# Ten embedding tables on one core: loads of five tiles of x, and pairs of tiles in the last table

## The chip, the cores and the metric

The kernel runs on one core of a Trainium2 chip. The metric is the device time of one execution in microseconds. Before the change it is 276.47 us, the median of three runs (276.41 to 276.67).

## The reference

Ten inputs x0 to x9 (1024 rows, 12500 down to 100 columns, float32) are multiplied by ten tables w0 to w9 (as many rows, 64 columns). The output holds, side by side, a factorization term over all tables and the ten products.

```python
embs = [jnp.dot(x, w) for x, w in zip(xs, ws)]
emb_sum = embs[0]
q_emb = jnp.dot(xs[0] ** 2, ws[0] ** 2)
for i in range(1, len(xs)):
    emb_sum = emb_sum + embs[i]
    q_emb = q_emb + jnp.dot(xs[i] ** 2, ws[i] ** 2)
fm_ans = 0.5 * (emb_sum ** 2 - q_emb)
return jnp.concatenate([fm_ans] + embs, axis=-1)
```

The elements of x are zeros and ones, nearly all of them zeros.

## The kernel before

x is kept transposed: a table with v rows is cut into tiles of 128 of them, and one tile of x is 128 partitions by the 1024 rows of the batch, 512 KB. There are 196 tiles. In memory the tiles of one table lie behind each other in each partition, so a load of n tiles is 128 rows of 4n KB each. The tiles go through a ring of 20 slots in SBUF (`x_ring`, `RING`, line 46).

`ORDER` (line 29) is written by hand. It names the tables in the order in which they are worked on (8, 9, 5, 4, 7, 3, 1, 6, 0, and 2 last), cuts each into groups of up to eight tiles, and each group into chunks of one or two tiles. A group is the unit in which w is loaded, squared and split into a high and a low part (`load_w`, `square` on ScalarE, lines 360 and 368; the split on GpSimd, lines 468 and 470). A chunk is the unit of ScalarE and TensorE: `count_set` (line 373) turns a chunk of x into zeros and ones (`is_set`) and counts them, `multiply` (line 497) multiplies it by the low and the high part of [w, w squared], four matmuls of 512 columns for a tile. The last group's last two tiles (`H`) are loaded in halves of the batch and are `FINAL`: the first of them goes the usual way in two half chunks, the second through `multiply_last` (line 515, six bf16 matmuls) and through ScalarE at line 420.

`plan_counts` (line 128) makes the loads and counts. It joins chunks of one group to at most four tiles (`LOAD`, line 45; two in the last table). Each joined list is one `Count`: VectorE's `count_ones` (line 601) counts the ones in it with one instruction. It is also one `Load`, except in the last table, where each chunk has a load of its own, and the four half loads of `FINAL`. A load gets a place in the ring: behind the one before it, or at slot 0 where it does not fit before slot 20 any more (line 152). `load.free` (line 173) is the count up to which ScalarE and VectorE must have read before the place, and the landing semaphore, may be used again.

SP issues the loads of x in their order at line 327, each behind its wait at line 325, and the outputs of nine tables behind them at line 333. w is loaded by ScalarE's queue at line 365. ScalarE's instructions stand in the order of the chunks, with the squarings, the copies of finished sums (`copy_sums`, line 390) and of finished embeddings (`copy_emb`, line 395) between them. At most five chunks are between ScalarE and TensorE (`SETS`).

When the last chunk is multiplied, VectorE adds its sums to the total (line 629), TensorE transposes total and sums (lines 554 and 527), ScalarE and VectorE make the first output from them, and a flag says whether all elements were zeros and ones (lines 564 to 569 on TensorE, 650 and 653 on VectorE). All engines read that flag before the program ends.

Of the kernel before, what the change touches and what calls it, by code (L numbers as in the profile page):

```python
# [16 lines left out]
BATCH = 1024  # L17
# [8 lines left out]

H = "halves"
FULL = [2, 2, 2, 2]
ORDER = [
    (8, [[2]]),  # L30
    (9, [[1]]),
    (5, [[2]]),
    (4, [[2, 2, 1]]),
    (7, [[2, 2]]),
    (3, [FULL, [2]]),
    (1, [FULL] * 6 + [[1]]),
    (6, [FULL]),
    (0, [FULL] * 12 + [[2]]),
    (2, [FULL, [2, 1, 1, 1, 1], [1, 1, 1, 1, H]]),
]  # L40
LAST = ORDER[-1][0]
CHUNK = max(FULL)
GROUP = sum(FULL)

LOAD = 4
# [14 lines left out]
class Chunk:  # L60


    def __init__(self, k, table, tile, n, at, half=None):
        self.k, self.table, self.tile, self.n, self.at = k, table, tile, n, at

        self.halves = (0, 1) if half is None else (half,)
        self.first, self.width = (half or 0) * HALF, len(self.halves) * HALF
        self.group = self.count = None
# [22 lines left out]
class Group:  # L91


    def __init__(self, g, place, table, tile, sizes, k):
        self.g, self.place, self.table, self.tile = g, place, table, tile
        self.whole, self.pair = g % WHOLES, g % PAIRS
        self.chunks, at = [], 0
        for n in sizes:
            if n == H:
                n = 2  # L100
                for half in range(2):
                    self.chunks.append(Chunk(k + len(self.chunks), table, tile + at, 1, at, half))
            else:
                self.chunks.append(Chunk(k + len(self.chunks), table, tile + at, n, at))
            at += n
        for chunk in self.chunks:
            chunk.group = self
        self.tiles, self.end = at, k + len(self.chunks)
# [3 lines left out]
def plan():  # L112
    groups, k = [], 0
    for n, (table, lists) in enumerate(ORDER):
        tile = 0
# [12 lines left out]
def plan_counts():  # L128

    lists = []  # L130
    for group in GROUPS:
        joined = []
        for chunk in group.chunks:
            most = 2 if group.table == LAST else LOAD
            if joined and (sum(c.n for c in joined) + chunk.n > most or
                           len(chunk.halves) < len(joined[0].halves)):
                lists.append(joined)
                joined = []
            joined.append(chunk)
        lists.append(joined)  # L140
    loads, counts, at = [], [], 0
    for chunks in lists:
        one = chunks[0]
        if len(one.halves) == 1:
            parts = [(one.tile, 1), (one.tile + 1, 1)]
        elif one.table == LAST:
            parts = [(chunk.tile, chunk.n) for chunk in chunks]
        else:
            parts = [(one.tile, sum(chunk.n for chunk in chunks))]
        length = sum(n for _, n in parts) * BATCH  # L150

        at = 0 if at + length > RING * BATCH else at
        own = []
        for first in range(0, BATCH, one.width):
            for i, (tile, n) in enumerate(parts):
                here = at + first + sum(m for _, m in parts[:i]) * BATCH
                own.append(Load(len(loads) + len(own), one.table, tile, n, first, one.width, here))
        at += length
        counts.append(Count(len(counts), own, chunks))
        place = own[0].at  # L160
        for chunk in chunks:

            chunk.place, place = place, place + chunk.n * chunk.width
            chunk.load = max((load for load in own if load.at < place), key=lambda load: load.at)
        for load in own:
            load.count = counts[-1]
        loads += own
    counts[-1].loads.sort(key=lambda load: load.at)
    for load in loads:

        had = [other.count for other in loads[:load.i] if other.land == load.land or
               other.at < load.at + load.length and load.at < other.at + other.length]
        load.free = max([count.c + 1 for count in had] + [0])
    return loads, counts


LOADS, COUNTS = plan_counts()

FINAL = COUNTS.pop()
# [8 lines left out]
def due(k, after):  # L188

    return [n for n in range(NT - 1) if min(END[n] - 1 + after, NCHUNKS - 1) == k]  # L190


def rec_kernel(nc, xs, ws, out):
# [3 lines left out]
    with ExitStack() as ctx:  # L197
# [120 lines left out]
        def _(sp):  # L318
# [11 lines left out]

            for n, (t, _) in enumerate(ORDER[:-1]):
                sp.wait_ge(emb_copied, n + 1)
# [26 lines left out]
        def _(act):  # L359
# [33 lines left out]
            def copy_emb(n, t):  # L393
                act.wait_ge(sums_turned, n + 1)
                nc.scalar.activation(results[:, t + 1, :, :], turning(n), ACT.Copy  # L395
                                     ).then_inc(emb_copied, 1)
# [6 lines left out]
            for group in GROUPS:  # L403
                for c, chunk in enumerate(group.chunks):
# [8 lines left out]
                    for n in due(chunk.k, TAKE_AFTER):  # L413
                        copy_emb(n, ORDER[n][0])

# [302 lines left out]
```

## Time and profile before

| what | value |
|---|---|
| runs, median (lowest to highest) | 276.47 us (276.41 to 276.67) |
| the profiled execution: time, span | 276.46 us, 274.7 us |
| PE, DVE, ACT, POOL busy | 78%, 82%, 82%, 42% of the span |
| DMA | 113.92 MB, mean 415 GB/s |
| loads of x | 42 of 2048 KB, 9 of 1024 KB, 11 of 512 KB, 4 of 256 KB |
| a count of four tiles, VectorE | 4.42 us |
| a chunk of two tiles, of one tile, ScalarE | 1.91 us, 1.06 us |

The span is the time from the first to the last record of the profile; the execution is 1.8 us longer. The busy shares are means over the whole span: three engines and the transfers are all busy most of it, so the shares alone do not say which of them sets the time. The slices and the waits do.

### The profile page before, as it was taken

The numbers are of one execution on the slowest core, as the hardware profiler recorded it, in microseconds if no ns is written. First come the engines' busy times: TensorE is split into PE (matmuls) and PEld (weight loads), VectorE is DVE, ScalarE is ACT, GpSimd is POOL, SyncE is SP. The second block draws the span as 40 slices with busy tenths as digits, with TensorE's granted clock in tenths as the row PEclk, the third lists the DMA queues.
The fourth block names the chain that finished last, engine by engine and source line by source line (L and its number), as shares of the span: only waits on it lengthen the run. The fifth ranks groups of instructions, "written<-read, shape, count | busy, mean of one in ns | idle before, by whom it ended". The sixth has DMA issues, their size and how long they took to land.

```text
span 274.7 us, 2715 instructions
## 1 busy us (share of the span) xinstructions
PE 213.9 (78%) x891; PEld 151.0 (55%) x892; DVE 224.1 (82%) x136; ACT 224.7 (82%) x269; POOL 114.9 (42%) x82
## 2 busy tenths in 40 slices
PE   0529889699988867878887787788788688698995
PEld 0416566476756555656654555555555465466763
DVE  2676876888798798878978978987987897999985
ACT  1649998999988788899868878877877796899994
POOL 0446757585414109267235135045045051073922
PEclk9968999999999999999999999999999999999999
DMA  7999999999999999999999999999999999999997
GB/s 263 441 402 440 410 420 417 426 421 442 416 424 426 427 420 426 421 423 428 420 424 430 420 431 428 417 424 429 420 427 431 419 423 430 410 414 416 410 398 269
DMA packets 15710, 113.92 MB, mean 415 GB/s; under 512 B 2000, under 2 KB 3280, under 8 KB 9168
## 3 DMA queue, kind: packets, MB, share of 16 engines
q1 hardware_dynamic: 11088, 106.96, 92.9%
q10 hardware_dynamic: 4608, 6.79, 6.7%
q8 instruction: 7, 0.11, 0.2%
q14 instruction: 7, 0.06, 0.1%
HBM read 110.85 MB, written 2.88 MB: 414 GB/s over the span
## 4 chain that ended last, share of the span: by engine, by line
DMA 63%; ACT 13%; issue 12%; PE 7%; SPq 1%; POOL 1%; ACTq 1%; DVE 0%; POOLq 0%
DMA x_ring<-in_x_dram 58%; ACT is_set L379 9%; PE sums L510 6%; DMA whole<-in_w_dram 5%; ACT turned L390 2%; SPq L327 1%; ACT whole L371 1%; POOL total L481 1%; ACT results L395 1%; ACTq L365 1%; PE sums L520 0%; ACT L371 0%; PE sums L554 0%; POOL high L468 0%; PE sums L527 0%
## 5 line engine op out<-in xcount | busy, mean ns | idle before, releaser
L604 DVE TENSOR_SCALAR_CACHE_REDUCE is_one<-x_ring 128x4096 uint8<-128x4096 f32 (+2 forms) x59 | 219.6, 3732 | 45.9 <-DMA x_ring<-in_x_dram 44.4
L379 ACT ACTIVATE is_set<-x_ring 128x2048 fp32r<-128x2048 uint32 (+2 forms) x106 | 190.1, 1796 | 32.1 <-DMA x_ring<-in_x_dram 31.6
L510 PE MATMUL sums<-is_set,low 128*128 128x512 f32 x396 | 133.1, 417 | 57.8 <-ACT is_set L379 42.8
L510 PE MATMUL sums<-is_set,high 128*128 128x512 f32 x396 | 124.9, 396 | 0.0
L510 PEld LDWEIGHTS sums<-is_set,low 128*128 128x128 f32 x396 | 68.1, 190 | 97.7 <-ACT is_set L379 43.3
L468 POOL CAST high<-whole 128x1024 fp32r<-128x1024 f32 (+5 forms) x31 | 27.1, 874 | 140.9 <-ACT whole L371 140.9
L510 PEld LDWEIGHTS sums<-is_set,high 128*128 128x128 f32 x396 | 75.5, 191 | 17.5
L470 POOL TENSOR_TENSOR low<-whole,high 128x1024 fp32r<-128x1024 f32 (+5 forms) x31 | 60.8, 1961 | 2.5
L371 ACT ACTIVATE whole<-whole 128x512 f32<-128x512 f32 (+5 forms) x31 | 16.5, 535 | 7.3 <-DMA whole<-in_w_dram 7.3
L379 ACT ACTIVATION_READ_ACCUMULATOR is_set<-x_ring 128x1 f32 x106 | 19.8, 187 | 0.0
L481 POOL TENSOR_TENSOR total<-total,turned 128x1024 f32<-128x1024 f32 x8 | 19.2, 2398 | 0.0
L390 ACT ACTIVATE turned<-sums 128x1024 f32<-128x1024 f32 x9 | 9.1, 1016 | 0.4 <-issue 0.3
L527 PEld LDWEIGHTS sums<-identity,turned 64*128 64x128 f32 x80 | 5.8, 139 | 3.9 <-issue 3.5
L527 PE MATMUL sums<-identity,turned 64*128 64x64 f32 x80 | 7.3, 229 | 0.0
L371 ACT ACT_TABLE_LOAD x1 | 1.3, 1283 | 6.1 <-DMA whole<-in_w_dram 6.1
L395 ACT ACTIVATE results<-sums 128x512 f32<-128x512 f32 x9 | 5.3, 585 | 0.0
L491 POOL TENSOR_SCALAR is_one<-x_ring 128x1024 bf16<-128x1024 f32 x1 | 2.8, 2784 | 5.1 <-DMA x_ring<-in_x_dram 5.1
L604 DVE DVE_READ_ACCUMULATOR is_one<-x_ring 128x1 f32 x59 | 4.9, 83 | 0.0
L448 POOL TENSOR_SCALAR total<-total,weight 128x1024 f32<-128x1024 f32 x1 | 2.9, 2863 | 0.1
L465 POOL COPY results<-whole 128x128 f32<-128x128 f32 x1 | 0.3, 292 | 4.3 <-ACT whole L371 4.3
L429 ACT ACTIVATE turned<-sums 128x512 f32<-128x512 f32 x2 | 1.2, 595 | 0.9 <-DVE total L629 0.9
L629 DVE SCALAR_TENSOR_TENSOR total<-sums,weight,total 128x512 f32<-128x512 f32 x2 | 1.5, 750 | 0.1
(37 smaller groups left out, 13.7 us busy)
## 6 DMA issues: line engine op xcount, KB each, us to landing
x_ring<-in_x_dram SPq DMA_DIRECT2D x42, 2048.0 KB, 21.5
x_ring<-in_x_dram SPq DMA_DIRECT2D x9, 1024.0 KB, 19.1
x_ring<-in_x_dram SPq DMA_DIRECT2D x11, 512.0 KB, 17.8
whole<-in_w_dram ACTq DMA_DIRECT2D x21, 256.0 KB, 9.7
out_dram<-results SPq DMA_DIRECT2D x9, 256.0 KB, 9.1
x_ring<-in_x_dram SPq DMA_DIRECT2D x4, 256.0 KB, 14.3
whole<-in_w_dram ACTq DMA_DIRECT2D x2, 192.0 KB, 7.1
whole<-in_w_dram ACTq DMA_DIRECT2D x4, 64.0 KB, 8.8
```

Of the source, the lines that this page charges most:

```text
L371: nc.scalar.activation(w[:, 1], w[:, 0], ACT.Square).then_inc(squared, 1)
L379: nc.scalar.activation(is_set[chunk.k % SETS][:, 0:length], in_ring(chunk.place, length).bitcast(U32), ACT.Sign, accum_out=set_counts[:, c ...
L390: nc.scalar.activation(turned[n % 2][:, :].rearrange("p (a b) -> p a b", a=2), sums[:, at:at + 2, :], ACT.Copy).then_inc(sums_copied, 1)
L395: nc.scalar.activation(results[:, t + 1, :, :], turning(n), ACT.Copy).then_inc(emb_copied, 1)
L448: nc.gpsimd.tensor_scalar(total[:, :], total[:, :], weight[:, 0:1], None, ALU.mult).then_inc(total_weighted, 1)
L468: nc.gpsimd.tensor_copy(first, w).then_inc(high_ready, 1)
L470: nc.gpsimd.tensor_tensor(part_of(group, low), w, first.bitcast(F32), ALU.subtract).then_inc(parts_ready, 1)
L481: nc.gpsimd.tensor_tensor(total[:, :], total[:, :], turned[n % 2][:, :], ALU.add).then_inc(added, 1)
L491: nc.gpsimd.tensor_scalar(last_ones[:, 0:BATCH], in_ring(FINAL.at, BATCH), 1.0, None, ALU.is_equal).then_inc(masked, 1)
L510: last = nc.tensor.matmul(sums[:, summing(n, half), :], w, x[:, at:at + HALF], start=first, stop=False, skip_group_check=True)
L527: last = nc.tensor.transpose(turning(n)[:, b, :], turned[n % 2][0:D, b * P:(b + 1) * P], identity[0:D, 0:D])
L604: nc.vector.tensor_scalar(is_one[c % 2][:, to:to + length], in_ring(at, length), 1.0, None, ALU.is_equal, ALU.add, accum_out=one_counts[:, ...
```

## The change

`FIVE` is a new list of sizes. A group of that shape is loaded in one transfer of five tiles. Its chunks stay 2, 2, 1, and it has two counts, one of four tiles and one of the fifth. The tables 4, 3, 1 and 0, which left one or two tiles over when cut by four, get one or two such groups at their end: table 3 is two of them, table 1 ends in a group of four and one of five, table 0 in two of five. In the last table a list of chunks is one load now, so the four pairs of one-tile chunks are each loaded in one transfer. The number of groups stays 31; there are 108 chunks in place of 106, 61 counts in place of 59 and 58 loads in place of 66.

```diff
--- before.py
+++ after.py
@@ -26,16 +26,17 @@
 
 H = "halves"
 FULL = [2, 2, 2, 2]
+FIVE = [2, 2, 1]
 ORDER = [
     (8, [[2]]),
     (9, [[1]]),
     (5, [[2]]),
-    (4, [[2, 2, 1]]),
+    (4, [FIVE]),
     (7, [[2, 2]]),
-    (3, [FULL, [2]]),
-    (1, [FULL] * 6 + [[1]]),
+    (3, [FIVE, FIVE]),
+    (1, [FULL] * 5 + [[2, 2], FIVE]),
     (6, [FULL]),
-    (0, [FULL] * 12 + [[2]]),
+    (0, [FULL] * 11 + [FIVE, FIVE]),
     (2, [FULL, [2, 1, 1, 1, 1], [1, 1, 1, 1, H]]),
 ]
 LAST = ORDER[-1][0]
@@ -94,7 +95,7 @@
     def __init__(self, g, place, table, tile, sizes, k):
         self.g, self.place, self.table, self.tile = g, place, table, tile
         self.whole, self.pair = g % WHOLES, g % PAIRS
-        self.chunks, at = [], 0
+        self.chunks, self.sizes, at = [], sizes, 0
         for n in sizes:
             if n == H:
                 n = 2
@@ -143,10 +144,17 @@
         one = chunks[0]
         if len(one.halves) == 1:
             parts = [(one.tile, 1), (one.tile + 1, 1)]
-        elif one.table == LAST:
-            parts = [(chunk.tile, chunk.n) for chunk in chunks]
         else:
             parts = [(one.tile, sum(chunk.n for chunk in chunks))]
+        if one.group.sizes == FIVE and one.at:
+
+            load = counts[-1].loads[0]
+            counts.append(Count(len(counts), [load], chunks))
+            counts[-1].at, counts[-1].length = load.at + one.at * BATCH, BATCH
+            one.place, one.load, load.count = counts[-1].at, load, counts[-1]
+            continue
+        if one.group.sizes == FIVE:
+            parts = [(one.tile, sum(FIVE))]
         length = sum(n for _, n in parts) * BATCH
 
         at = 0 if at + length > RING * BATCH else at
@@ -157,6 +165,8 @@
                 own.append(Load(len(loads) + len(own), one.table, tile, n, first, one.width, here))
         at += length
         counts.append(Count(len(counts), own, chunks))
+        if one.group.sizes == FIVE:
+            counts[-1].length = LOAD * BATCH
         place = own[0].at
         for chunk in chunks:
```

The names in the rows below: `x_ring` is the ring, `in_x_dram` the inputs, `is_set` a chunk after ScalarE, `x_landed` the landing semaphores (`LANDS`, 16 of them by turns). 128x4096 is four tiles, 128x1024 one.

SP's queue, the loads of x, before:

```order
L327 DMA x_ring<-in_x_dram 128x2048
L327 DMA x_ring<-in_x_dram 128x4096 x12
L327 DMA x_ring<-in_x_dram 128x1024
L327 DMA x_ring<-in_x_dram 128x4096 x26
L327 DMA x_ring<-in_x_dram 128x2048 x6
L327 DMA x_ring<-in_x_dram 128x1024 x8
L327 DMA x_ring<-in_x_dram 128x512 x4
L333 DMA out_dram<-results 128x512 x9
```

and now:

```order
L337 DMA x_ring<-in_x_dram 128x5120 x2
L337 DMA x_ring<-in_x_dram 128x4096 x11
L337 DMA x_ring<-in_x_dram 128x5120
L337 DMA x_ring<-in_x_dram 128x4096 x24
L337 DMA x_ring<-in_x_dram 128x5120 x2
L337 DMA x_ring<-in_x_dram 128x2048 x9
L337 DMA x_ring<-in_x_dram 128x512 x4
L343 DMA out_dram<-results 128x512 x9
```

The loads of one and two tiles at the ends of the tables 3, 1 and 0 (and 4, further up) are gone into loads of five. The last table has nine loads of two tiles where it had five of two and eight of one.

ScalarE at the end of table 0 and the begin of the last table, before:

```order
L379 ACTIVATE is_set,set_counts<-x_ring 128x2048 [waits x_multiplied,x_landed15]
L371 ACTIVATE whole<-whole 128x512 [waits w_landed1]
L379 ACTIVATE is_set,set_counts<-x_ring 128x2048 [waits x_multiplied,x_landed15]
L379 ACTIVATE is_set,set_counts<-x_ring 128x2048 [waits x_multiplied,x_landed0]
L365 DMA whole<-in_w_dram 128x384 [waits parts_ready]
L371 ACTIVATE whole<-whole 128x384 [waits w_landed2]
L379 ACTIVATE is_set,set_counts<-x_ring 128x2048 [waits x_multiplied,x_landed1]
```

and now:

```order
L389 ACTIVATE is_set,set_counts<-x_ring 128x2048 [waits x_multiplied,x_landed10]
L389 ACTIVATE is_set,set_counts<-x_ring 128x2048 [waits x_multiplied,x_landed11] x2
L375 DMA whole<-in_w_dram 128x384 [waits parts_ready]
L389 ACTIVATE is_set,set_counts<-x_ring 128x1024 [waits x_multiplied,x_landed11]
L381 ACTIVATE whole<-whole 128x512 [waits w_landed1]
L389 ACTIVATE is_set,set_counts<-x_ring 128x2048 [waits x_multiplied,x_landed12] x2
L375 DMA whole<-in_w_dram 128x384 [waits parts_ready]
L389 ACTIVATE is_set,set_counts<-x_ring 128x1024 [waits x_multiplied,x_landed12]
L381 ACTIVATE whole<-whole 128x384 [waits w_landed2]
L389 ACTIVATE is_set,set_counts<-x_ring 128x2048 [waits x_multiplied,x_landed13]
```

Before, table 0 ended in two chunks of one load and one chunk of a load of its own. Now its last two loads have three chunks each, all three of a load wait for the same semaphore, and a chunk of one tile has come in at each.

ScalarE in the last table, the chunks of one tile and the halves, before:

```order
L379 ACTIVATE is_set,set_counts<-x_ring 128x1024 [waits x_multiplied,x_landed6]
L379 ACTIVATE is_set,set_counts<-x_ring 128x1024 [waits x_multiplied,x_landed7]
L379 ACTIVATE is_set,set_counts<-x_ring 128x1024 [waits x_multiplied,x_landed8]
L379 ACTIVATE is_set,set_counts<-x_ring 128x1024 [waits x_multiplied,x_landed9]
L379 ACTIVATE is_set,set_counts<-x_ring 128x1024 [waits x_multiplied,x_landed10]
L379 ACTIVATE is_set,set_counts<-x_ring 128x1024 [waits x_multiplied,x_landed11]
L379 ACTIVATE is_set,set_counts<-x_ring 128x1024 [waits x_multiplied,x_landed12]
L379 ACTIVATE is_set,set_counts<-x_ring 128x1024 [waits x_multiplied,x_landed13]
L379 ACTIVATE is_set,set_counts<-x_ring 128x512 [waits x_multiplied,x_landed14]
L379 ACTIVATE is_set,set_counts<-x_ring 128x512 [waits x_multiplied,x_landed0]
```

and now:

```order
L389 ACTIVATE is_set,set_counts<-x_ring 128x1024 [waits x_multiplied,x_landed2] x2
L389 ACTIVATE is_set,set_counts<-x_ring 128x1024 [waits x_multiplied,x_landed3] x2
L389 ACTIVATE is_set,set_counts<-x_ring 128x1024 [waits x_multiplied,x_landed4] x2
L389 ACTIVATE is_set,set_counts<-x_ring 128x1024 [waits x_multiplied,x_landed5] x2
L389 ACTIVATE is_set,set_counts<-x_ring 128x512 [waits x_multiplied,x_landed6]
L389 ACTIVATE is_set,set_counts<-x_ring 128x512 [waits x_multiplied,x_landed8]
```

Before, every chunk of one tile waited for a semaphore of its own. Now two of them wait for one. The chunks and the halves behind them are the same.

## Rows read from the trace of the kernel before

**Rows 1.** The page's slices: DMA busy in tenths, and GB/s, 40 equal slices.
```profile
DMA  7999999999999999999999999999999999999997
GB/s 263 441 402 440 410 420 417 426 421 442 416 424 426 427 420 426 421 423 428 420 424 430 420 431 428 417 424 429 420 427 431 419 423 430 410 414 416 410 398 269
```
**Rows 2.** The page's DMA queues: packets, MB, share of 16 engines' span.
```profile
q1 hardware_dynamic: 11088, 106.96, 92.9%
q10 hardware_dynamic: 4608, 6.79, 6.7%
```
**Rows 3.** The page's chain that ended last, by engine.
```profile
DMA 63%; ACT 13%; issue 12%; PE 7%; SPq 1%; POOL 1%; ACTq 1%; DVE 0%; POOLq 0%
```
**Rows 4.** Timeline of VectorE, last table: start us, us, instruction, idle before it.
```profile
251.69 2.29 DVE L604 TENSOR_SCALAR_CACHE_REDUCE is_one<-x_ring 128x2048 uint8<-128x2048 f32 x1
...
254.19 2.29 DVE L604 TENSOR_SCALAR_CACHE_REDUCE is_one<-x_ring 128x2048 uint8<-128x2048 f32 x1 [0.20 <-DMA x_ring<-in_x_dram]
...
256.82 2.29 DVE L604 TENSOR_SCALAR_CACHE_REDUCE is_one<-x_ring 128x2048 uint8<-128x2048 f32 x1 [0.34 <-issue]
...
261.94 2.29 DVE L604 TENSOR_SCALAR_CACHE_REDUCE is_one<-x_ring 128x2048 uint8<-128x2048 f32 x1 [0.27 <-issue]
...
264.51 2.29 DVE L604 TENSOR_SCALAR_CACHE_REDUCE is_one<-x_ring 128x2048 uint8<-128x2048 f32 x1 [0.27 <-issue]
```
**Rows 5.** Timeline of ScalarE, end of table 0 and last table.
```profile
227.95 1.91 ACT L379 ACTIVATE is_set<-x_ring 128x2048 fp32r<-128x2048 uint32 x1 [1.19 <-DMA x_ring<-in_x_dram]
...
238.38 1.92 ACT L379 ACTIVATE is_set<-x_ring 128x2048 fp32r<-128x2048 uint32 x1 [1.14 <-DMA x_ring<-in_x_dram]
...
244.60 0.51 ACT L371 ACTIVATE whole<-whole 128x384 f32<-128x384 f32 x1
245.02 1.91 ACT L379 ACTIVATE is_set<-x_ring 128x2048 fp32r<-128x2048 uint32 x1
...
257.39 1.06 ACT L379 ACTIVATE is_set<-x_ring 128x1024 fp32r<-128x1024 uint32 x1
...
258.43 1.05 ACT L379 ACTIVATE is_set<-x_ring 128x1024 fp32r<-128x1024 uint32 x1
...
260.58 1.06 ACT L379 ACTIVATE is_set<-x_ring 128x1024 fp32r<-128x1024 uint32 x1
...
263.14 1.06 ACT L379 ACTIVATE is_set<-x_ring 128x1024 fp32r<-128x1024 uint32 x1
...
264.43 1.06 ACT L379 ACTIVATE is_set<-x_ring 128x1024 fp32r<-128x1024 uint32 x1
...
265.49 0.61 ACT L379 ACTIVATE is_set<-x_ring 128x512 fp32r<-128x512 uint32 x1
```
**Rows 6.** Timeline of TensorE, the end, and VectorE's last instruction.
```profile
265.64 0.72 PE L510 MATMUL sums<-is_set,low 128*128 128x512 f32 x2
...
266.67 0.39 PE L510 MATMUL sums<-is_set,low 128*128 128x512 f32 x1
...
268.30 0.59 PE L510 MATMUL sums<-is_set,low 128*128 128x512 f32 x1
...
269.12 0.63 PE L554 MATMUL sums<-identity,total 128*128 128x128 f32 x4
...
271.59 0.19 PE L569 MATMUL sums<-ones,odd_sum 128*1 128x1 f32 x2
...
272.52 0.14 DVE L653 CAST odd_flag<-flag_sum 1x1 int32<-1x1 f32 x1
```
**Rows 7.** The start: ScalarE, VectorE and SP's issues, from their timelines.
```profile
17.50 1.90 ACT L379 ACTIVATE is_set<-x_ring 128x2048 fp32r<-128x2048 uint32 x1
...
5.86 2.29 DVE L604 TENSOR_SCALAR_CACHE_REDUCE is_one<-x_ring 128x2048 uint8<-128x2048 f32 x1 [3.49 <-DMA x_ring<-in_x_dram]
...
15.14 4.42 DVE L604 TENSOR_SCALAR_CACHE_REDUCE is_one<-x_ring 128x4096 uint8<-128x4096 f32 x1 [2.87 <-DMA x_ring<-in_x_dram]
...
58.59 4.42 DVE L604 TENSOR_SCALAR_CACHE_REDUCE is_one<-x_ring 128x4096 uint8<-128x4096 f32 x1 [1.16 <-DMA x_ring<-in_x_dram]
...
0.81 3.52 SPq L327 DMA_DIRECT2D x_ring<-in_x_dram  x7
...
53.52 4.64 SPq L327 DMA_DIRECT2D x_ring<-in_x_dram  x2
```

## The prediction

> **What bounds the kernel now.** I read the slices first. From the second slice to the last but one the 16 DMA engines are busy nine tenths or more and move between 398 and 442 GB/s [rows 1]: the transfers never stop, so the stream of x and w is the bound, and an engine that idles costs nothing as long as the stream goes on. The queue rows say the same: x and the outputs take 92.9% of the engines' time, w and one output 6.7% [rows 2]. The chain of waits agrees as far as the stream lasts, 63% of it is DMA, but it also has PE in it [rows 3], and that part lies at the end. So there are two things to price: how long the stream is, and what comes between its last tiles and the end of the program.
>
> The end is read from the timelines. In the last table a load of one tile lands about every 1.28 us and ScalarE takes each as it comes: it starts on a tile at 263.14 and at 264.43 [rows 5]. That last one-tile chunk (chunk 103) reaches TensorE at 265.64, 1.21 us after ScalarE began it. From there TensorE has work without a gap: the four matmuls of that chunk, those of the first half of the last tiles at 266.67, the six bf16 ones, the other half at 268.30, the transposes from 269.12, the flag's matmuls until 271.8; the flag is turned to an integer at 272.52, two microseconds before the end [rows 6]. From 265.64 on, what delays TensorE delays the end by as much.
>
> **What the change takes away.** Eight loads fewer: one each in tables 4, 3, 1 and 0, four in the last. The bytes are the same, so only the share of a load that does not depend on its size goes. Call a tile's bytes u and that share v. Three readings:
> - VectorE counts pairs of one-tile loads as they land, at 256.82 and 264.51, three pairs in 7.69 us [rows 4], so u + v = 1.282 us. Just before, a load of two tiles takes 254.19 - 251.69 = 2.50 us [rows 4], so 2u + v = 2.50 and v = 0.064.
> - ScalarE waits for a load of four tiles at 227.95 and, two loads later, at 238.38 [rows 5]. Those 10.43 us hold eight tiles and one w load of 256 KB, half a tile's bytes: 8.5u + 3v = 10.43. With u + v = 1.282, v = 0.085.
> - By queue: 11088 packets and 106.96 MB take 92.9% of 16 x 274.7 us, 4608 packets and 6.79 MB take 6.7% [rows 2]. The two equations give 26.8 bytes per ns and 8.9 ns a packet. A load is 128 rows and, as the packet totals need (16 more for each of 77 and 32 DMAs), 16 small packets: 9 on an engine, v = 0.080.
>
> I take 0.075, between them: 8 x 0.075 = **0.60 us** (0.50 to 0.68). All eight loads lie ahead of the last four transfers, so the last pair of full tiles lands 0.60 us earlier.
>
> **What it adds.** The pair of tiles 16 and 17 of the last table is one load now, so tile 16 is not there 1.28 us ahead: both come at 264.43 - 0.60 = 263.83. Nothing else about these chunks changes; ScalarE still takes them as two chunks of one tile. Back to back such chunks start 1.04 us apart (257.39, 258.43), and before a half chunk 1.06 (264.43, 265.49) [rows 5]. So the second one starts **1.05 us** after the landing where it started at it. Behind it the run of TensorE is as long as before: the half chunks are on ScalarE's side earlier than TensorE comes to them (0.6 us a chunk against TensorE's 1.03), and the last four transfers, unchanged in size, land 0.60 us earlier too. TensorE's last run begins 1.05 - 0.60 = 0.45 us later, and the end with it.
>
> **What costs nothing, and its cover.**
> - In tables 3 and 0 ten tiles are six chunks and not five: two of 1.04 us for one of 1.9, +0.2 us of ScalarE each. In table 3 the ring covers it, in table 0 the backlog below counts it. VectorE counts a load of five in two steps, +0.15 us in each of these tables; it waits for x there.
> - A load of five lands its first four tiles one tile's time later. At the start this is 15.14 + 1.2 = 16.4 us for table 4, and ScalarE does not come to that chunk before 17.50, since it waits for w [rows 7].
> - The ring. The tightest place before is the load issued at 53.52 [rows 7]; the tile ahead of it in the queue is counted from 58.59, so 5 us of transfers are still queued. The change keeps that distance (12 tiles from the oldest tile not yet read to the new one). A new tight place comes at the end of table 0: the first load of five does not fit behind slot 16 and goes to slot 0, so it waits for loads 39 and 40, with only 41 and 42 behind them: 8 tiles, 9.8 us, less the 4.4 us in which VectorE counts load 40 [rows 7]: over 5 us still queued. The first load of all was counted 5.1 us after its issue, its own 2.5 us of transfer in it, so a gap is not to be feared; if it came, it would cost its length.
> - SP issues eight times less; it waits most of the time anyway.
>
> **Is ScalarE there in time?** It is the place where the sum could break. Table 0's last five tiles land at once. Before, 96 tiles of it were there at 238.38 and twelve more by 254.19 [rows 4, 5]: two of them make 2.64 us, so tile 98 landed at 241.0, now 0.3 earlier, 240.7. From there two chunks of 1.9, one of 1.04 and a squaring (0.42, from 244.60 to 245.02 [rows 5]) bring ScalarE to 245.96, where it began the last table at 245.02 before. From that point to tile 14 of the last table it does the same work without waiting, 260.58 - 245.02 = 15.56 us: 261.52 now. The pair of tiles 14 and 15 was counted from 261.94 [rows 4] and lands 6 x 0.075 = 0.45 earlier, at 261.49. Two chunks later it is 263.6, and the last pair comes at 263.83. So ScalarE, 0.9 us later than before, has caught up with 0.2 us to spare.
>
> **Sum**, against the profiled execution (276.46 us, span 274.7; the median of the runs, 276.47, is the same): -0.60 + 1.05 = +0.45, **276.9 us**. With the ends of the terms +0.36 to +0.56: 276.8 to 277.0. A difference under 0.2%, 0.55 us, can't be told from none here, so faster means under 275.9 and slower over 277.0.
>
> **A rule against the row.** The per-load share stands on rows alone: 0.064 to 0.085 us. The Trainium skill (DMA: Bandwidth & Descriptors, section "Why small descriptors are slow (HBM only)") gives a packet a fixed cost of about three cycles of the DMA engine's inner bus. With the 850 MHz that its section "Where 436 GB/s comes from" names for the fabric, 9 packets are 0.03 us a load, an estimate; eight loads would bring 0.25 us, and the sum by it would be +0.8. The packet rows disagree (8.9 ns each, not 3.5), and the measurement decides.
>
> **The rivals.**
> - *The tail is hidden, wholly or in part (faster).* If the last stores or the flag's path, not TensorE, set the end, or TensorE makes up the later start, the shorter stream is all that is left: -0.50 to -0.68, 275.8 to 276.0; partly hidden, up to 276.6. For it: most of the chain is DMA. Against it: the unbroken run from 265.64. The Trainium skill (Perfetto Trace Analysis, "DMA Optimizations") calls larger transfers the main remedy where DMA bounds, which by itself would be this case. 0.20, of which 0.13 below 275.9.
> - *ScalarE does not catch up (slower).* 0.2 us of slack rests on a landing that no row shows. If tile 98 lands 0.3 us later, or TensorE holds up a copy, every tenth beyond comes on top: 277.1 to 277.7, at the middle 277.4. It decides once ScalarE finishes tile 15 after the last pair has landed. 0.13.
> - *Loads of five bring nothing.* No row shows one. If a row of 20 KB is moved in two packets, the four pairs alone save 4 x 0.064 = 0.25, and the sum is +0.8: 277.3. The change would then not do what it says to the transfers. The rule of the section above gives about the same figure. 0.07.
>
> **Numbers.** The forecast has 0.60: 0.42 of it within 0.2%, 0.18 above, since 277.0 lies inside its reach. Faster 0.13, same 0.42 + 0.07 = 0.49, slower 0.18 + 0.13 + 0.07 = 0.38. The range 276.1 to 277.5 takes in the forecast, the partly hidden tail, loads of five that bring nothing and most of the late ScalarE; about 0.14 is left out, most of it the wholly hidden tail.
>
> **What would show it.** Right: the slices as full as before; the last pair counted at about 263.9 instead of 264.51; two chunks of 1024 on ScalarE back to back, the second with no wait; TensorE's last run from about 266.1 and its transposes from 269.6. Wrong: TensorE starting that run at 265.1 or so (hidden tail), ScalarE never waiting for x between tiles 10 and 17 (late), or the last full tiles landing at 264.2 (loads of five bring nothing). A slice with fewer than nine tenths would say that the ring ran dry.

## The result, and the profile after

The change is slower: 280.7 us in the median of six runs (four of them 278.89 to 282.27), beside 276.44 us before on the same chip; the ratio is 1.012, interval 1.0088 to 1.0153. Two of the six took 696 and 1109 us for a cause that no trace here shows, and are left out of the ratio, which compares means; the other four have a median of 279.1. The forecast was 276.9 us, at most 277.5. The profiled execution took 278.89 us with a span of 277.2: 2.43 us more than before, and its rows account for that.

The page of the changed kernel, its clock and DMA slices, its queues and its chain:

```profile
PEclk9975999999999997999999999999999999799999
DMA  7999999999999999999999999999999999999996
GB/s 264 424 425 452 395 378 346 416 416 419 423 425 427 436 416 422 430 429 422 416 429 428 424 425 421 431 427 422 425 430 416 424 434 428 408 419 419 426 394 229
...
q1 hardware_dynamic: 9936, 106.96, 92.3%
q10 hardware_dynamic: 4608, 6.79, 6.6%
...
DMA 61%; ACT 15%; issue 13%; PE 7%; POOL 1%; ACTq 1%; DVE 1%; SPq 0%; POOLq 0%
```

Against [rows 1] three slices stand out, the fifth to the seventh (28 to 49 us): 395, 378 and 346 GB/s where before every slice from the second to the last but two has 402 or more. The busy digit is 9 all the same, so it is the GB/s that must be read. The queue has 1152 packets fewer than in [rows 2], eight loads of 144, and the chain is shaped as in [rows 3]. The windows say when the stream thinned out. First before:

```profile
32.00:60.00 28.00, 23.94 (x111) 16.97 (x109) 21.33 (x11) 26.75 (x33) 19.66 (x13) 1.00 1.02 425
```

and the change (PE, PEld, DVE, ACT, POOL busy, then clock, DMA share, GB/s):

```profile
32.00:36.00 4.00, 3.58 (x21) 2.43 (x20) 3.01 (x5) 4.00 (x8) 2.43 (x3) 1.00 0.95 341
...
44.00:48.00 4.00, 3.73 (x20) 2.67 (x20) 2.64 (x3) 4.00 (x8) 1.86 (x3) 1.00 0.85 285
...
32.00:60.00 28.00, 24.57 (x118) 17.27 (x117) 20.61 (x14) 28.00 (x38) 19.24 (x12) 1.00 0.98 386
```

39 GB/s less over 28 us are 1.09 MB, 2.6 us at 425 GB/s. And ScalarE, idle for 1.25 of the 28 us before, is now busy in all of them: it is behind. The start of its timeline says since when:

```profile
9.07 0.33 ACTq L375 DMA_DIRECT2D whole<-in_w_dram  x1
...
19.50 0.47 ACT L381 ACTIVATE whole<-whole 128x320 f32<-128x320 f32 x1 [7.36 <-DMA whole<-in_w_dram]
...
20.78 1.90 ACT L389 ACTIVATE is_set<-x_ring 128x2048 fp32r<-128x2048 uint32 x1
...
25.52 0.42 ACT L381 ACTIVATE whole<-whole 128x256 f32<-128x256 f32 x1 [2.75 <-DMA whole<-in_w_dram]
...
26.75 1.90 ACT L389 ACTIVATE is_set<-x_ring 128x2048 fp32r<-128x2048 uint32 x1
```

The same rows before:

```profile
9.05 0.33 ACTq L365 DMA_DIRECT2D whole<-in_w_dram  x1
...
16.22 0.47 ACT L371 ACTIVATE whole<-whole 128x320 f32<-128x320 f32 x1 [4.26 <-DMA whole<-in_w_dram]
...
20.55 0.42 ACT L371 ACTIVATE whole<-whole 128x256 f32<-128x256 f32 x1 [1.06 <-DMA whole<-in_w_dram]
...
21.78 1.90 ACT L379 ACTIVATE is_set<-x_ring 128x2048 fp32r<-128x2048 uint32 x1
```

The w of table 4 (160 KB) is issued at the same time and lands 3.28 us later. ScalarE works in its written order, and the squaring of that w stands ahead of the chunk of table 5 (17.50 in [rows 7], 20.78 now); the next w is late too, and table 4's first chunk starts at 26.75 instead of 21.78. Five microseconds late, ScalarE frees the ring late. SP's issues of the loads that begin with tiles 28, 32 and 36 of the stream, before

```profile
34.76 0.33 SPq L327 DMA_DIRECT2D x_ring<-in_x_dram  x1
...
39.87 0.33 SPq L327 DMA_DIRECT2D x_ring<-in_x_dram  x1
...
44.66 0.33 SPq L327 DMA_DIRECT2D x_ring<-in_x_dram  x1
```

and with the change:

```profile
39.17 0.33 SPq L337 DMA_DIRECT2D x_ring<-in_x_dram  x1
...
45.81 0.33 SPq L337 DMA_DIRECT2D x_ring<-in_x_dram  x1
...
51.64 0.33 SPq L337 DMA_DIRECT2D x_ring<-in_x_dram  x1
```

VectorE counts a load when it has landed, and shows the hole:

```profile
46.60 4.42 DVE L614 TENSOR_SCALAR_CACHE_REDUCE is_one<-x_ring 128x4096 uint8<-128x4096 f32 x1 [1.36 <-DMA x_ring<-in_x_dram]
54.42 4.42 DVE L614 TENSOR_SCALAR_CACHE_REDUCE is_one<-x_ring 128x4096 uint8<-128x4096 f32 x1 [3.40 <-DMA x_ring<-in_x_dram]
```

The load issued at 45.81 is the one counted at 54.42; the one ahead of it had landed by 46.60. So at most 0.8 us of transfers were queued at its issue, where [rows 7] had 5 at the tightest place, and the queue ran dry: the two counts lie 7.8 us apart, where before they lie 5.6 to 6.8 apart from 40 to 59 us.

The end, first on ScalarE:

```profile
264.49 1.05 ACT L389 ACTIVATE is_set<-x_ring 128x1024 fp32r<-128x1024 uint32 x1
...
265.93 1.06 ACT L389 ACTIVATE is_set<-x_ring 128x1024 fp32r<-128x1024 uint32 x1 [0.31 <-DMA x_ring<-in_x_dram]
...
266.99 1.04 ACT L389 ACTIVATE is_set<-x_ring 128x1024 fp32r<-128x1024 uint32 x1
```

then on TensorE (first half chunk, transposes) and VectorE:

```profile
269.20 0.39 PE L520 MATMUL sums<-is_set,low 128*128 128x512 f32 x1
...
271.54 0.63 PE L564 MATMUL sums<-identity,total 128*128 128x128 f32 x4
```

```profile
265.93 2.29 DVE L614 TENSOR_SCALAR_CACHE_REDUCE is_one<-x_ring 128x2048 uint8<-128x2048 f32 x1
...
274.95 0.14 DVE L663 CAST odd_flag<-flag_sum 1x1 int32<-1x1 f32 x1
```

As forecast, the last pair comes at once, its two chunks run back to back, and the second has no wait. From the landing of the last full tile to the half chunk on TensorE are 269.20 - 265.93 = 3.27 us; in [rows 5, 6] 266.67 - 264.43 = 2.24. That is 1.03 us more. The rest of the 2.43 is the stream: the last pair came 1.4 us later (265.93 against 264.51 in [rows 4]) instead of 0.6 earlier.

### The profile page after: what moved, and what is told of

Read it like the earlier page. It is cut to its first block, busy times and chain, and to the rows that moved or that the text cites. A ratio compares the mean times of both kernels' runs of the same rounds, so it can differ in the third digit from the quotient of the medians.

```text
span 277.2 us, 2713 instructions
## 1 busy us (share of the span) xinstructions
PE 216.2 (78%) x892; PEld 154.4 (56%) x892; DVE 223.8 (81%) x140; ACT 224.2 (81%) x273; POOL 114.9 (41%) x82
## 4 chain that ended last, share of the span: by engine, by line
DMA 61%; ACT 15%; issue 13%; PE 7%; POOL 1%; ACTq 1%; DVE 1%; SPq 0%; POOLq 0%
DMA x_ring<-in_x_dram 56%; ACT is_set L389 11%; DMA whole<-in_w_dram 6%; PE sums L520 5%; ACT whole L381 2%; ACT turned L400 1%; ACT results L405 1%; ACTq L375 1%; POOL low L480 1%; PE sums L530 0%; ACT L381 0%; PE sums L564 0%; PE sums L537 0%; POOL high L478 0%; DVE flag_sum L660 0%
## 5 line engine op out<-in xcount | busy, mean ns | idle before, releaser
L520 PE MATMUL sums<-is_set,high 128*128 128x512 f32 x396 | 126.7, 401 | 0.0
L520 PEld LDWEIGHTS sums<-is_set,low 128*128 128x128 f32 x396 | 70.0, 194 | 96.5 <-ACT is_set L389 37.0
L520 PEld LDWEIGHTS sums<-is_set,high 128*128 128x128 f32 x396 | 76.6, 194 | 17.7
L389 ACT ACTIVATION_READ_ACCUMULATOR is_set<-x_ring 128x1 f32 x108 | 20.4, 189 | 0.0
## 6 DMA issues: line engine op xcount, KB each, us to landing
x_ring<-in_x_dram SPq DMA_DIRECT2D x11, 1024.0 KB, 16.4
```

The lines of the kernel that those rows point to most:

```text
L389: nc.scalar.activation(is_set[chunk.k % SETS][:, 0:length], in_ring(chunk.place, length).bitcast(U32), ACT.Sign, accum_out=set_counts[:, c ...
L520: last = nc.tensor.matmul(sums[:, summing(n, half), :], w, x[:, at:at + HALF], start=first, stop=False, skip_group_check=True)
```

## The experiments

All were run in five rounds against the kernel before on the same chip, whose median there was 277.0 us for the first four experiments and 276.47 to 276.51 for the others. The diffs show only the lines that matter. Where a diff puts table 4 back to `[2, 2, 1]`, the kernel also has `is FIVE` in place of `== FIVE`: the two lists are equal, so with `==` that table would still get one load of five. Line numbers differ by a few. At the end of this section a table parts each kernel's profiled execution into stream and end.

**Pairs alone.** The four tables as before, the last table's pairs as in the change.

```diff
-    (4, [FIVE]),
+    (4, [[2, 2, 1]]),
-    (3, [FIVE, FIVE]),
-    (1, [FULL] * 5 + [[2, 2], FIVE]),
+    (3, [FULL, [2]]),
+    (1, [FULL] * 6 + [[1]]),
-    (0, [FULL] * 11 + [FIVE, FIVE]),
+    (0, [FULL] * 12 + [[2]]),
```

> Only the pairs of the last table; tables 4, 3, 1 and 0 are loaded as before. Theory A (the loss of the change has two parts: about 2.1 us at the start, where w comes late and the ring runs dry, and 1.05 us at the end, where the last pair serializes two chunks on ScalarE): the start is as before, four loads fewer bring 0.25 to 0.3 us, the end costs 1.05, so 276.44 + 0.75 = 277.2 us; no slice under 390 GB/s before the end; TensorE's last run begins 1.05 us later against the landing. Rival B (the loads of five cost all of it, each its share, by their place in the ring, and the end is hidden): 276.2 us.

Measured: 277.61 us, ratio 1.0018 (1.0009 to 1.0026). No thin slice (none under 411 GB/s from the second to the last but two). The end costs what the change's end costs: 268.15 - 264.87 = 3.28 us, TensorE's half chunk after the landing.

**Fives alone.** The last table loaded as before.

```diff
+        elif one.table == LAST:
+            parts = [(chunk.tile, chunk.n) for chunk in chunks]
```

> Only the loads of five; the last table has its one-tile loads back. Theory A: the start as in the change (w of table 4 lands at 19.5 us, slices of 346 to 395 GB/s between 32 and 48 us, 2.1 us lost), the end as before, four loads fewer bring 0.3 us: 276.44 + 1.8 = 278.2 us. Rival B: nearly all of the loss stays, 278.9 to 279.1 us.

Measured: 280.49 us, ratio 1.013 (1.0099 to 1.016), more than was expected. The whole loss is with the loads of five:

```profile
GB/s 243 439 420 431 412 323 356 386 421 409 424 425 431 420 430 421 427 424 420 430 430 417 429 426 426 424 425 426 417 426 426 428 431 425 407 419 414 410 397 270
```

**Fives in tables 1 and 0 only.** Pairs stay, tables 4 and 3 as before.

```diff
-    (4, [FIVE]),
+    (4, [[2, 2, 1]]),
-    (3, [FIVE, FIVE]),
+    (3, [FULL, [2]]),
```

> Pairs in the last table and loads of five in tables 1 and 0 alone; tables 4 and 3 are loaded as before (4 and 1; 4, 4 and 2). Theory A: w of table 4 lands at 16.2 again, no slice under 390 GB/s at the start; six loads fewer bring 0.45, the end costs 1.05: 276.44 + 0.6 = 277.0 us. Rival B: three of the six loads of five are left, so half of the 2.1 us stays, plus what the ring's hole at the end of table 0 costs: 277.5 to 278.1 us.

Measured: 277.79 us, ratio 1.0025 (1.0016 to 1.0033). No thin slice; the w of table 4 lands at 16.51. The loss is in the early tables.

**The change, but table 4 in four and one.** One line undone.

```diff
-    (4, [FIVE]),
+    (4, [[2, 2, 1]]),
```

> The change, but table 4 is loaded in 4 and 1 as before; tables 3, 1 and 0 keep their loads of five. Theory A in its narrow form (w of table 4 is late because it shares the DMA engines, row by row, with rows of 16 and 20 KB where it had the 4 KB rows of a one-tile load beside it): that w lands at 16.2 again, ScalarE takes table 4's first chunk at 17.5, most of the 2.1 us is back: 277.0 to 277.5 us. Wide form (any larger rows ahead of any w cost): table 3's loads of five still hold up the w after it, about 278 us. Rival B: 278.7 to 279 us.

Measured: 277.47 us, ratio 1.0018 (1.0005 to 1.0031). With that one load of five gone the thin slices are gone, and w lands early again. From the page and from ScalarE's timeline:

```profile
GB/s 239 435 418 436 413 420 424 421 424 429 420 423 425 436 418 422 418 431 429 421 429 421 423 426 431 419 428 422 419 431 429 423 429 419 418 416 421 419 398 222
...
16.56 0.47 ACT L381 ACTIVATE whole<-whole 128x320 f32<-128x320 f32 x1 [4.13 <-DMA whole<-in_w_dram]
```

**The kernel before, with table 4 in one load of five.** The converse. The diff is against the kernel before; the planning code of the change is in it too.

```diff
-    (4, [[2, 2, 1]]),
+    (4, [FIVE]),
```

> The kernel before with one edit: table 4's five tiles in one load. One load fewer, the last table and the other tables as before. Theory A: the whole of the start's loss is here, w of table 4 at 19.5 us or later, ratio 1.005 to 1.010 (1.5 to 2.8 us slower), the end as before. Rival B: one of six loads of five, a sixth of the loss, ratio 1.001 to 1.002.

Measured: 279.74 us, ratio 1.0109 (1.0094 to 1.0123). Nothing but this load differs from before, and it costs 3.3 us, a little more than expected:

```profile
GB/s 265 424 421 420 281 431 428 421 420 422 417 424 432 424 419 427 425 422 418 422 431 421 430 433 419 429 426 419 424 423 426 426 426 419 412 418 414 410 398 211
...
19.61 0.47 ACT L383 ACTIVATE whole<-whole 128x320 f32<-128x320 f32 x1 [7.43 <-DMA whole<-in_w_dram]
```

**The change, with table 4's w issued at the start.** It goes to a place of its own in `results` (free that early), right behind the first three w, at 2.2 us instead of 9.07. Of the edit only the loop that issues it is shown:

```diff
-            for group in GROUPS[:AHEAD]:
+            for group in GROUPS[:AHEAD + 1]:
                 load_w(group)
```

> The change with all its loads of x; only w of table 4 goes to a place of its own (a part of the output buffer that is written late) and is issued at the start with the first three w loads instead of behind ScalarE's first chunk. Theory A (the loss at the start is ScalarE waiting for w of table 4, and behind it for that of table 7): the waits of 7.4 and 2.8 us shrink to under 2 us together, no slice under 390 GB/s at the start, and what is left is what splitting table 4's load left, ratio 1.002 to the kernel before, 0.4 to 0.6 us slower. Rival B (the loads of five in the ring cost it: their place, or that five tiles must be read before one is issued): ScalarE waits less but the dips between 32 and 48 us stay, ratio 1.008 to 1.012.

Measured: 276.75 us, ratio 1.0021 (1.001 to 1.0031), six runs at 276.56 to 276.75 and five at 277.39 to 277.80. Most of the loss is gone, though all loads of five are there, so most of it was not these loads' place in the ring. But it is not gone in the way expected: in the profiled execution (277.63, one of the five) a slice of 381 GB/s is left, and ScalarE still waits:

```profile
17.29 0.47 ACT L389 ACTIVATE results<-results 128x320 f32<-128x320 f32 x1 [5.05 <-DMA results<-in_w_dram]
```

That is 15 us from issue to use for 160 KB. By the DMA records of the trace, 7.8 of them pass before w's first row begins, while the same queue still moves the three w ahead of it, and 6.1 from its first row to its last. Counting the records by size shows why the rows take so long. Below are rows begun in each microsecond on all 16 DMA engines together, w of table 4 (1280 bytes a row) and x, by the trace's raw clock, which runs about 11 us ahead of the timelines here; in brackets the size of the x rows.

```
raw us                    21  22  23  24  25  26  27  28  29
before     w               0   0  12  18  84  14   0   0   0
           x [16, 4 KB]   27  21  30  18  63  78  19  29  19
before,    w               0   0   3  19  22  35  22  23   4
4 in five  x [20, 16 KB]  25  22  16  22  22  20  19  29  22
change,    w               8  25  22  17  16  21  19   0   0
w early    x [20, 16 KB]  16  24  21  19  16  16  31  17  32
```

While w has rows, about as many of them go as rows of x. In the kernel with w early the rows of w can be counted off in sets of 16, one for each engine, and the sets begin 0.82 us apart (the second 0.89 after the first): a row of x of 20 KB, 767 ns in the median, and a row of w, 55 ns, are 0.82. So each engine takes one row of either queue by turns. Before, 84 of the 128 went in the one microsecond in which x was the 4 KB rows of table 4's fifth tile. Without that load each row of w stands behind 20 or 16 KB. A 4 KB row takes 161 ns in the median of the kernel before, one of 16 KB 615.

**Table 4 in three and two.** The kernel before otherwise, 66 loads; table 4's chunks are of one, two and two tiles then.

```diff
-    (4, [[2, 2, 1]]),
+    (4, [[1, 2, 2]]),
```

> The kernel before with table 4 in a load of three tiles and one of two in place of four and one; nothing else differs, 66 loads. Theory A (w is served row by row beside x, so the length of the x rows that run beside it decides when it lands): rows of 12 and 8 KB in place of 16 and 4, w of table 4 lands at 15.0 to 16.3, no later than before (16.2), ScalarE's idle time at the squaring no longer, ratio 0.999 to 1.001. Theory B (only the short 4 KB rows of the one-tile load let w through): w lands at 17 to 18, half of the way to the 19.6 of the run with table 4 in one load, and the ratio is 1.003 to 1.006.

Measured: 276.98 us, ratio 1.0034 (1.0009 to 1.0059), runs from 276.33 to 279.98. The w lands at 16.97, later than theory A says (15.0 to 16.3) and almost where theory B has it (17 to 18), whose ratio (1.003 to 1.006) is met too:

```profile
16.97 0.47 ACT L371 ACTIVATE whole<-whole 128x320 f32<-128x320 f32 x1 [5.20 <-DMA whole<-in_w_dram]
```

The turns hold even so: in raw microseconds 24, 25 and 26 there are 40, 46 and 32 rows of w beside 43, 44 and 33 of 8 KB. So rows of 8 KB let w through as well, against the wording of theory B. Theory A erred in that w's rows begin only some 3.5 us after the issue (raw 23), so the 12 KB rows hardly mattered. With 4, 8 and 20 KB rows at the end of table 4, w lands at 16.22, 16.97 and 19.6.

**Is it TensorE's clock?** In the run of fives alone the clock was at the lower level from 20 to 32 us:

```profile
20.00:32.00 12.00, 7.59 (x23) 5.69 (x24) 10.09 (x7) 9.25 (x12) 7.45 (x6) 0.50 1.02 429
```

The same kernel with 28 more matmuls on the identity while TensorE waits:

```diff
+                for _ in range({2: 24, 3: 4}.get(group.g, 0)):
+                    nc.tensor.matmul(sums[:, 6, 0:P], identity[:, :], identity[:, :], start=True,
+                                     stop=True, skip_group_check=True)
```

> The kernel with only the loads of five (ratio 1.013), with 24 small matmuls of the identity on TensorE ahead of table 5's chunk and 4 ahead of table 4's, into a bank that is written only at the end: they fill the 8 us in which TensorE waits at the start. Their result is not used. Theory A with the clock (that kernel lost 1.4 us more at the start than the change did, because TensorE's granted clock stayed at half to 32 us in place of 28): the granted clock is 1.00 from 20 to 32 us, ratio 1.006 to 1.009. Without the clock in it: the granted clock is 1.00 and the ratio stays 1.011 or more.

Measured: 279.97 us, ratio 1.012 (1.0102 to 1.0139), as without them (1.013). The clock was 0.86 there, not the 1.00 that was expected, and the stream as thin as in the change:

```profile
20.00:32.00 12.00, 8.22 (x41) 6.10 (x42) 10.08 (x7) 9.24 (x12) 7.47 (x6) 0.86 1.02 428
32.00:60.00 28.00, 24.63 (x117) 17.26 (x117) 21.22 (x15) 28.00 (x38) 19.04 (x12) 1.00 0.98 385
```

A clock near that of before (0.87 in this stretch) gave nothing back, so the clock is not what the change lost by.

**What is left to gain?** Four kernels had table 4 as before and kept the last pair of full tiles apart. First, the tables 1 and 0 in fives, table 3 as before and three pairs joined:

```diff
+        elif chunks[-1].k == NCHUNKS - 3:
+            parts = [(chunk.tile, chunk.n) for chunk in chunks]
```

> Loads of five in tables 1 and 0 alone, pairs in the last table but for the last one (tiles 16 and 17 are two loads again): five loads fewer than before. Theory A: the start and the end as before, only the saving is left, 5 x 0.075 = 0.38 us, ratio 0.9986. If ScalarE does not catch up behind table 0's last load of five, 0.2 to 0.6 us comes back: ratio 0.999 to 1.001. Rival B: slower, 1.001 or more.

Measured: 276.70 us, ratio 1.0016 (1.0008 to 1.0025): a miss. The stream was shorter, but ScalarE ran without a pause from 261.24 to the end. To tell whether table 0's fives or the pairs made that, table 0 went back to what it was:

```diff
-    (0, [FULL] * 11 + [FIVE, FIVE]),
+    (0, [FULL] * 12 + [[2]]),
```

> Four loads fewer than before: table 1 ends in a group of four tiles and a load of five, and the first three pairs of one-tile chunks of the last table are one load each. The last pair of full tiles stays two loads, and the tables 4, 3 and 0 are as before. Theory A (a load taken away is worth 0.064 to 0.085 us as long as no w load at the start stands behind rows of 20 KB, ScalarE has caught up by tile 16 of the last table, and tile 16 comes ahead of tile 17): 0.26 to 0.34 us less, ratio 0.9987 to 0.9991; the last full pair counted 0.3 earlier against the first count, and the half chunk on TensorE as far behind it as before. Theory B (ScalarE, not the stream, sets the end as soon as the pairs of the last table come in one load, whatever table 0 ends in): ScalarE has no wait from tile 10 to 17 and the ratio is 1.000 to 1.002.

Measured: 276.72 us, ratio 1.0007 (0.9998 to 1.0016), not the 0.9987 to 0.9991 of theory A. The pairs do it without table 0's fives:

```profile
261.51 1.06 ACT L391 ACTIVATE is_set<-x_ring 128x1024 fp32r<-128x1024 uint32 x1 [0.29 <-DMA x_ring<-in_x_dram]
...
262.56 1.04 ACT L391 ACTIVATE is_set<-x_ring 128x1024 fp32r<-128x1024 uint32 x1
...
263.61 1.05 ACT L391 ACTIVATE is_set<-x_ring 128x1024 fp32r<-128x1024 uint32 x1
...
264.65 1.04 ACT L391 ACTIVATE is_set<-x_ring 128x1024 fp32r<-128x1024 uint32 x1
```

ScalarE waits for tiles 14 and 15, which come together, and then has four chunks of 1.05 us to do. Tile 17 is there at 264.15 by VectorE's count; ScalarE begins it at 264.65, later than before (264.43 in [rows 5]). A joined pair puts ScalarE 1.05 us back, and it makes good only 2.57 - 2.09 = 0.48 us in the next pair's time. Table 3 in fives as well:

```diff
-    (3, [FULL, [2]]),
+    (3, [FIVE, FIVE]),
```

> The run before with table 3 as two loads of five as well: five loads fewer than before. Theory A: 0.32 to 0.43 us less, ratio 0.9984 to 0.9988, the w of tables 4 and 7 landing as before (16.2 and 20.6), no slice under 390 GB/s between the second and the last but one. Theory B (rows of 20 KB hold up a w wherever they stand, in table 3 that of table 1's first groups): ScalarE waits over 2 us more for whole than before, a slice under 390 between 20 and 60 us, ratio 1.002 to 1.010.

Measured: 276.78 us, ratio 1.002 (1.0007 to 1.0033), again not the saving of theory A. Rows of 20 KB in table 3 cost nothing at the start (no thin slice), against its theory B; the end is longer still, 8.79 us against 8.45 in the kernel just above, and why is open. Last, of the pairs only tiles 10 and 11 joined:

```diff
-        elif chunks[-1].k == NCHUNKS - 3:
+        elif one.table == LAST and chunks[0].k > NCHUNKS - 9:
```

> The run with the tables 3 and 1 in loads of five, but of the last table's one-tile chunks only the first two (tiles 10 and 11) in one load; the other six have loads of their own, as before. Three loads fewer than before. Theory A (the last run showed the stream 0.4 to 0.5 us shorter with five loads fewer, and gave it back because ScalarE takes 1.045 us for each of the four one-tile chunks from the landing of tiles 14 and 15 on; with these two apart it has caught up by tile 14): every one-tile chunk from tile 14 on starts at its landing, the last one 0.2 to 0.3 us earlier than before, and so the end: ratio 0.9989 to 0.9993. Theory B (the last table's pairs were not what gave it back, but the loads of five ahead of them, or TensorE): the last one-tile chunk no earlier than before, or the end no earlier than it was although that chunk is: ratio 0.9998 to 1.002.

Measured: 276.44 us against 276.51; ratio 1.0011 (0.9998 to 1.0025), ten runs at 276.20 to 276.85 and two at 278.0 and 278.1. The ratio of theory A (0.9989 to 0.9993) is missed. The profiled run is the shortest seen, 276.20 us, and its last one-tile chunk starts 0.47 us earlier than before (264.43), more than the 0.2 to 0.3 expected:

```profile
263.96 1.06 ACT L391 ACTIVATE is_set<-x_ring 128x1024 fp32r<-128x1024 uint32 x1
...
268.88 0.63 PE L566 MATMUL sums<-identity,total 128*128 128x128 f32 x4 [0.22 <-DVE total L641]
```

Of the 0.47 us, 0.22 go in a new wait of TensorE for VectorE's addition of the last sums. Three loads fewer are worth some 0.25 us in the profile, and the comparison cannot tell that from nothing: no version here is measurably faster than the kernel before.

The table: loads, from VectorE's first count to its count of the last pair of full tiles (stream), from there to its last instruction (end), both in us in the profiled execution, and the ratio of the runs.

| kernel | loads | stream | end | ratio |
|---|---|---|---|---|
| before | 66 | 258.65 | 8.01 | 1 |
| change | 58 | 260.06 | 9.02 | 1.012 |
| pairs alone | 62 | 258.34 | 9.02 | 1.0018 |
| fives alone | 62 | 261.33 | 8.36 | 1.013 |
| pairs, fives in 1 and 0 | 60 | 258.29 | 9.34 | 1.0025 |
| change, table 4 in four and one | 59 | 257.84 | 9.03 | 1.0018 |
| before, table 4 in five | 65 | 262.05 | 8.02 | 1.0109 |
| change, w early | 58 | 258.64 | 9.02 | 1.0021 |
| before, table 4 in three and two | 66 | 259.66 | 8.00 | 1.0034 |
| fives alone, 28 more matmuls | 62 | 260.77 | 8.37 | 1.012 |
| three pairs, fives in 1 and 0 | 61 | 257.96 | 8.80 | 1.0016 |
| three pairs, five in 1 | 62 | 258.11 | 8.45 | 1.0007 |
| three pairs, fives in 3 and 1 | 61 | 257.98 | 8.79 | 1.002 |
| one pair, fives in 3 and 1 | 63 | 258.22 | 8.23 | 1.0011 |

## Why the prediction was wrong

**The step that failed** is "A load of five lands its first four tiles one tile's time later. At the start this is 15.14 + 1.2 = 16.4 us for table 4, and ScalarE does not come to that chunk before 17.50, since it waits for w". The landing was right, 16.36 by VectorE's count. But the cover was taken as fixed: w's own landing hung on the rows of x beside it, and moved from 16.22 to 19.50. The row at 17.50 was also misread; it is table 5's chunk, and table 4's first came at 21.78. The step priced a change of one queue against a wait on the other as if they did not share the engines. It was costed at nothing and cost some 2.0 us of the stream (the last pair landed at 265.93 against the forecast 263.9) in the change, 3.3 us of the time by itself.

**The ring**, "The change keeps that distance", fell with it. It kept its 12 tiles, as the step said, but not the 5 us of queued transfers: ScalarE came 5 us late, and 0.8 us were left. "A gap is not to be feared" looked only at the places where the change shifts slots.

**A load's share**, 0.075 us, was of the right size. The rows of the kernel before give it a second time: four rows of 4 KB take 4 x 161 = 644 ns, one of 16 KB 615, so about 10 ns go with each row, and the eight rows that a load has on each engine are 0.08 us. Seven kernels without the loss at the start (pairs alone, pairs with fives in 1 and 0, table 4 in four and one, and the four with the last pair apart) have 34 loads fewer in all and streams 3.81 us shorter in all: 0.11 a load, from 0.06 to 0.14. That is rather more than forecast, but all seven are set against one profiled execution of the kernel before.

**The end**, 1.05 us, was right: 1.03 in the change, and the end is 9.02 to 9.03 us in four of the five kernels that have these pairs, against 8.01 before (9.34 in the fifth, where VectorE's addition waits 1.27 us for TensorE, and why is open). With it and the loads' share the sum holds within 0.2 us where the start is left alone: table 4 in four and one, seven loads fewer, gives -0.53 + 1.05 = +0.52, and measured +0.47 (277.47 against 277.0); pairs alone, four fewer, +0.75 and +0.61; pairs with fives in 1 and 0, six fewer, +0.60 and +0.79.

**ScalarE in time.** It waited 0.31 us for the last pair, as the step said; in the run with table 4 in four and one, whose stream is not late, 0.30 at 264.17. So that rival was not what happened. But the runs of three pairs showed what the step did not say: behind a joined pair ScalarE is late for the next two tiles.

**The rivals.** The tail was not hidden: all of it showed in the time. The third rival's condition did not hold: a row of 20 KB went as one packet (1152 packets fewer are eight loads of 144). What the loads of five bring in time the runs do not settle: beside the pairs alone, two such savings shortened the profiled stream by 0.05 us, three by 0.50. That a load of five delays another queue's transfer, none of the rivals had. The chance of slower was 0.38, and nearly all of it stood on 277.0 to 277.7.

What stays open: why the same late w costs 2.0 us in one kernel and 3.3 in another; why several kernels, that of three and two among them, have a few runs 1 to 3 us above the others; and the two long runs. To the first the traces give a place: in the kernel before with table 4 in five, the four tiles issued at 22.96 had landed by 32.42 and the next load came at 32.49, so the queue was empty already there; in the change, five tiles were issued at 22.86, had landed by 34.75, and the next load came at 33.14. That this makes the whole difference is not shown.

## What to carry to other kernels

Where a transfer on one queue is to be covered by a wait for another queue's, ask first whether the two share the engines: the cover moves with it. Merging loads saves about a tenth of a microsecond each in the traces here, which no version turned into a time measurably below the one before, and costs the first consumer its early tile. So merge in the middle of a stream, not ahead of a small load that an in-order engine waits for, nor at the end where every chunk is waited for. In a page whose DMA digits all read 9, look at the GB/s.

## What the runs showed of the hardware

Two queues with work were served about row for row, with x rows of 4, 8, 16 and 20 KB: beside x rows of 20 and 16 KB the 128 rows of a 160 KB w took six microseconds (raw 23 to 29), beside rows of 4 KB most of them took one. The Trainium skill (DMA: Bandwidth & Descriptors, section "Queues, rings and completion order") has each DMA engine take turns between queue rows by packets of typically 9 to 17 descriptors; the traces agree on the turns, but the turn here was a single row, by the sets of 16 rows begun 0.82 us apart.

A row of 20 KB went as one DMA record of 767 ns, 26.7 bytes per ns; rows of 16 KB took 615 ns, 26.6 bytes per ns. So the larger row is no slower by itself.
